# Cross-attention maxima pass from the keys' high parts, two heads on two halves of the array's rows

## The reference, cut to what matters

```python
q = (query @ w_q).reshape(B, Q, HEADS, HEAD_DIM).transpose(0, 2, 1, 3)
k = (key @ w_k).reshape(B, Kl, HEADS, HEAD_DIM).transpose(0, 2, 1, 3)
v = (value @ w_v).reshape(B, Kl, HEADS, HEAD_DIM).transpose(0, 2, 1, 3)
scores = jnp.einsum('bhqd,bhkd->bhqk', q, k) * scale
attn = jax.nn.softmax(scores, axis=-1)
out = jnp.einsum('bhqk,bhkd->bhqd', attn, v)
```

## Time and profile before

| what | value |
|---|---|
| three runs | 1546.65, 1551.68 and 1551.09 us, median 1551.09 |
| span of the profiled execution | 1543.7 us; its own time is not listed beside it, and the three runs are 3.0 to 8.0 us longer than this span |
| TensorE matmuls busy | 1382.7 us (90%) |
| VectorE busy | 1007.9 us (65%) |
| ScalarE busy | 886.8 us (57%) |
| GpSimd busy | 232.3 us (15%) |

### The profile page before, as it was taken

The page is one execution under the profiler, slowest core; times in us unless marked ns, Lnnn a source line. Parts: engine busy times, 40 slices in busy tenths (PEclk is TensorE's granted clock), DMA queues, the critical chain, the costliest instruction groups (busy, mean ns, idle before and its releaser), DMA issues. The chain is left out here.

```text
span 1543.7 us, 23087 instructions
## 1 busy us (share of the span) xinstructions
PE 1382.7 (90%) x8543; PEld 1040.3 (67%) x8543; DVE 1007.9 (65%) x1283; ACT 886.8 (57%) x1569; POOL 232.3 (15%) x214
## 2 busy tenths in 40 slices
PE   3999999999999998999999999999995999999653
PEld 3878786877777786877787777878783456355322
DVE  5657677685867676667767685767765656025376
ACT  3858576675758575757667585857661433023053
POOL 3202122120302111112112030211213000000000
PEclk9999999999999999999999999999996979569786
DMA  4000000000000013000000000000004151510000
GB/s 139 15 1 18 12 7 18 1 17 1 18 1 14 18 29 92 8 5 14 18 1 19 1 18 2 18 14 1 4 1 153 19 70 17 61 13 1 20 1 14
DMA packets 31717, 34.64 MB, mean 22 GB/s; under 512 B 2688, under 2 KB 28800, under 8 KB 31360
## 3 DMA queue, kind: packets, MB, share of 16 engines
q1 hardware_dynamic: 31616, 33.17, 9.5%
HBM read 25.82 MB, written 0.52 MB: 17 GB/s over the span
## 5 line engine op out<-in xcount | busy, mean ns | idle before, releaser
L459 DVE TENSOR_TENSOR prob_sum<-prob_sum,probs 128x1024 f32<-128x1024 f32 x224 | 264.5, 1222 | 164.6 <-ACT probs L382 163.9
L382 ACT ACTIVATE probs<-scores_a 128x1024 f32<-128x1024 f32 x128 | 131.2, 1025 | 209.1 <-PE scores_a L573 208.1
L311 POOL TENSOR_TENSOR k_split<-prob_sum,k_split 64x512 fp32r<-64x512 f32 x128 | 165.1, 1290 | 297.9 <-ACT prob_sum L358 297.9
L440 DVE TENSOR_REDUCE step_max<-scores_a 128x2 f32<-128x1024 f32 x128 | 156.9, 1226 | 35.4 <-PE scores_a L561 33.5
L440 DVE TENSOR_REDUCE step_max<-scores_b 128x2 f32<-128x1024 f32 x128 | 155.7, 1216 | 0.0
L572 PE MATMUL scores_a<-q_twice,k_split 128*128 128x256 f32 x512 | 139.2, 305 | 5.0 <-ACT q_low_max L373 4.9
L382 ACT ACTIVATE probs<-scores_b 128x1024 f32<-128x1024 f32 x128 | 131.3, 1026 | 0.0
L572 PE MATMUL scores_b<-q_twice,k_split 128*128 128x256 f32 x512 | 128.4, 283 | 0.0
L573 PE MATMUL scores_b<-q_low_max,k_ones 128*128 128x256 f32 x512 | 127.9, 282 | 0.0
L573 PE MATMUL scores_a<-q_low_max,k_ones 128*128 128x256 f32 x512 | 127.9, 283 | 0.0
L304 POOL TENSOR_TENSOR w_lo<-w_raw,w_hi 128x768 fp32r<-128x768 f32 x16 | 34.9, 2183 | 606.3 <-ACT w_hi L327 606.3
(11 more groups left out here) (210 smaller groups left out, 2784.1 us busy)
## 6 DMA issues: line engine op xcount, KB each, us to landing
ctx_rows<-in_ctx_dram SPq DMA_DIRECT2D x10, 512.0 KB, 3.7
grouped<-dots_sb SPq DMA_DIRECT2D x32, 136.0 KB
w_raw<-in_L_xattn_w_v_dram SPq DMA_DIRECT2D x14, 256.0 KB, 3.2
probs<-in_ctx_dram SPq DMA_DIRECT2D x6, 512.0 KB, 6.0
grouped<-dots_sb SPq DMA_DIRECT2D x32, 72.0 KB
w_raw<-in_L_xattn_w_q_dram SPq DMA_DIRECT2D x16, 128.0 KB, 2.4
w_raw<-in_L_xattn_w_k_dram SPq DMA_DIRECT2D x16, 128.0 KB, 2.4
wo_pair<-in_L_xattn_w_o_dram SPq DMA_DIRECT2D x16, 128.0 KB, 2.1
```

The costliest lines, as they stand in the source:

```text
L311: pool.tensor_tensor(k_split[0:DH, B, keys], k_staged_b[j % 2], k_split[DH:P, B, keys].bitcast(F32), ALU.subtract).then_inc(k_low[B], 1)
L382: act.activation(probs[:, j % 2, h, :], flat_scores[h], ACT.Exp, scale=SCALE).then_inc(exp_done, 1)
L440: dve.tensor_reduce(step_max[:, :, 1 - h, j - 1], scores[h][:, :, :], X, ALU.max).then_inc(max_done, 1)
L459: dve.tensor_tensor(prob_sum[:, h, :], prob_sum[:, h, :], probs[:, j % 2, h, :], ALU.add).then_inc(sum_done, 1)
```

## The change

The maxima pass multiplies only the high parts of queries and keys: head A on rows 0 to 63, head B on rows 64 to 127, where the high part of its keys lies. The matmuls are issued as A, B for the first half of the queries and A, B for the second. All waits stand ahead of the four matmuls: the pass waits for the high parts of the chunk (k_high) instead of the low ones, and for the reductions of both heads. The wait for the low parts moves to the first call of scores_by_keys for each head. Empty lines are left out of the diff.

```diff
             def scores_for_max(it, j):
                 keys = slice(j * CHUNK, (j + 1) * CHUNK)
+                pe.wait_ge(k_high, 2 * (STEPS * it + j) + 2)
                 for h in (A, B):
-                    pe.wait_ge(k_low[h], STEPS * it + j + 1)
                     if j > 0:
                         pe.wait_ge(max_done, 2 * (STEPS * it + j - 1) + h + 1)
                     else:
                         wait_past(pe, exp_done, 2 * STEPS * it)
-                    for qt in range(QT):
-                        last = mm(scores[h][:, qt, :], q_twice[:, h, qt * P:(qt + 1) * P], k_split[:, h, keys],
+                for qt in range(QT):
+                    for h in (A, B):
+                        rows = slice(h * DH, (h + 1) * DH)
+                        last = mm(scores[h][:, qt, :], q_twice[rows, h, qt * P:(qt + 1) * P], k_split[rows, h, keys],
                                   start=True, stop=True)
-                    last.then_inc(pre_made, 1)
+                        if qt == QT - 1:
+                            last.then_inc(pre_made, 1)
 
             def scores_by_keys(it, j, h):
 
                 if j > 0:
                     pe.wait_ge(exp_done, 2 * (STEPS * it + j - 1) + h + 1)
+                else:
+                    pe.wait_ge(k_low[h], STEPS * (it + 1))
                 for t in range(KT):
```

## The result

The changed kernel took **1574.17 us** in the median of 4 runs (1568.85 to 1575.44); the kernel before, on the same chip, 1548.87 (4 runs, 1526.43 to 1551.68). The ratio is 1.0203, with an interval of 1.0116 to 1.0290: slower, by some 25 us. The forecast was 1563, 12 us slower. The sign and the mechanism came out as forecast; the size was over twice the forecast one, and this part is about the other half. The ratios given in this document leave out the slower executions of each kernel, so they are not always the quotients of the medians beside them.

A forecast was written before the change was run, and what follows sets the result against it. TensorE sets most of the pace, in a loop with VectorE's reductions; 14 pairs at +0.85 us (11.9) and +0.1 in each of two first pairs give +12 on the 1551.1 median: 1563 us, range 1547 to 1575.

The forecast's parts named there:

- The bound, and the loop: Cross-attention pair: TensorE busy 32.70 of 34.00 us; scores banks refill only after their last reduction, which VectorE's next reduction needs.
- part 1: Scores for the maxima: A's and B's half-row matmuls run side by side, 0.47 us instead of 0.93.
- The rival without overlap: Scores for the maxima: A's and B's matmuls do not run at once; 1603 us, +52; chance 0.07.
- part 2: Array's division changes before and after each step's scores, 0.20 us each way; one call 0.87 us instead of 0.93.
- The rival in which row changes are free: Scores for the maxima: changing only rows costs nothing; 1543.7 us, faster; chance 0.12.
- the bound step of the walk: Where the reduction loop binds, one step takes 2.36 + 0.05 + 0.76 = 3.17 us, +0.06 in three steps.
- the walk: Step-by-step sum through one pair, between starts of A's reductions: last reductions +1.55 us, transpose of the maxima +0.85 us.
- steps 4 and 5: Fourth and fifth intervals between A's reductions in a pair: 3.69 us each, +0.34 and -0.06.
- part 4: Wait on k_low moves to the first scores_by_keys, k_high replaces it; neither binds, costed at nothing.
- the narrower value projection: Last pair of each batch: about the same loss as other pairs, counted in 14 x 0.85 = 11.9 us.
- a cheaper division: A division change costing less than 0.15 us, down to nothing: chance 0.30, 0.12 faster and 0.18 no difference.
- step 7: Last interval between A's reductions in a pair: the refill stands between them, 3.17 us instead of 2.27, +0.90.

The follow-up runs named there:

- run 5: The kernel before, with each reduction reading half of the scores (256 of 512 keys of each bank); 1520.85 us, one run.
- run 6: The changed kernel, with each reduction reading half of the scores; 1516.76 us, one run.
- run 7: The kernel before, full rows, with half a value projection between head A's and head B's scores from chunk 2 on; 1520.14 us, ratio 0.9857.
- run 9: The kernel of run 7 with both heads' scores on half rows, each head's two matmuls alone between value projections; 1600.37 us, one run.
- run 4: The changed kernel with one wait on the reductions (head B's, which includes A's) instead of two; 1578.49 us, ratio 1.0240.
- run 8: The changed kernel with the waits for the keys' low parts moved ahead of the transposes of the maxima; 1551.11 us, one run.
- run 1: The changed kernel with the last pair of each batch projecting its values at full width, 256 columns; 1556.65 us.
- run 3: The changed kernel, still on half rows, with the order and reduction waits of the kernel before; 1566.35 us, ratio 1.0128.
- run 2: The kernel before, on all 128 rows, with the change's order A, B, A, B and both heads' waits ahead; 1556.09 us, ratio 1.0054.

## Why the prediction was right or wrong

**The bound, and the loop: right.** The pair is set by the loop between the scores' banks and the reductions. Runs 5 and 6 take VectorE's part of the loop out, and the loss goes; run 7 hides the loop, and the pair gets 1.1 us shorter than before.

**The overlap (part 1): right.** The pairs start together, 402.07 and 402.08. The rival without overlap is out.

**The change of division (part 2): right, 0.20 forecast, 0.19 to 0.20 measured** in run 9, although it was read from changes of columns. In the changed kernel's rows the first reduction comes when forecast: the key projection's last matmul would have let the next start at 401.52 + 2 x 0.233 = 401.99, and 402.84 - 401.99 = 0.85 us, the forecast's own figure. The rival in which row changes are free is out with it. The Trainium skill (TensorEngine Tiling (Array Packing), Key Properties) says that a change of tiling mode drains the engine. The trace agrees in that each change costs 0.19 to 0.20 us, less than the forecast's estimate of 0.28 us for a full drain; that it is a drain, no run here shows. The Trainium skill (TensorEngine Tiling (Array Packing), Theoretical Speedup) gives up to twice for such a contraction; here two row pairs start 0.33 us apart where four full-row matmuls started 0.233 apart, and with both changes one call takes 0.85 instead of 0.93 us.

**The restart after a wait (the bound step of the walk): wrong in size.** The forecast took 0.05 + 0.76 = 0.81 us from the end of B's reduction to the next of A's. Measured: 0.15 + 0.74 = 0.89 (405.19, 405.34, 406.08). Its ground for part 2, that an empty array has nothing to drain, held: restarts with a change of division take as long as the late ones without (run 4). What failed is the 0.05, which was read at 403.52 in an ordinary pair of the kernel before, where the weight load carries the wait. The change puts more waits in front of the matmuls, and the one that ends last became an instruction of its own. The same trace had that price in its first pair, at 46.76. The four bound steps exceed the walk by 0.07 to 0.08 each, steps 4 and 5 by 0.04 and 0.02. Counted from 401.99, where the scores would have started without a change, the transpose comes after 28.01 us, where the forecast had 27.65: 0.36 more.

**The wait that moved (part 4): wrong.** "I cost it at nothing; the cover is the value projection." The cover held for the data, but not for the wait: 1.61 instead of 1.50 us from the transpose to the first scores by keys in every ordinary pair, 0.11 more, which run 8 finds between the release and the matmul. Both misses are one: the forecast priced waits by whether their data is there, and not by where they stand in TensorE's queue. An ordinary pair so loses 0.85 + 0.36 + 0.11 = 1.3 instead of 0.85. (The 0.85 hold the change in front of the first scores, 0.09 of which shows as 33.19 - 27.94 = 5.25 us from the first key projection to the first scores, where it was 5.16.)

**"With the narrower value projection the same walk gives about the same": wrong.** With wide projections and at a full clock these two pairs take 27.84 us from the scores to the transpose (run 1), as the others do; with the narrow ones it was 30.43. The forecast read a granted clock of 1.00 in the kernel before and took it as fixed, though the change thins TensorE's work. In the two last pairs it fell to the lower level, which cost 10.5 us in all. Seven kernels had half rows. Of these, the clock fell in both last pairs in the changed kernel and runs 3, 4 and 8, in one in run 9, and in none in run 1 (wider projections) and run 6 (short reductions, one wait left in such a pair). In the kernel before and in runs 2, 5 and 7, with full rows, it stayed. So it fell only where half rows and narrow projections came together, and not everywhere there; what decides is open, since in run 9 it fell without a wait just ahead and in run 6 it did not fall.

**The sum.** 15.3 in the 12 ordinary pairs, 10.5 for the clock and 2.0 for the rest of the two last pairs, 1.3 in the two first pairs, -0.6 at the start: 28.5 up to the end of the cross-attention, and +25 in the medians; the forecast's own terms gave 12. The range (1547 to 1575) held 1574.17 by a hair, and not by its reasons: it was widened by a cheaper division and by other small prices, while the clock was in none of its cases. Its 0.3% for what a measurement of this kernel tells was too small as well: the four runs of the kernel before lie between 1526.43 and 1551.68 us.

**After the transpose: nearly right.** Apart from the added wait, a pair's second stage takes as long as before (32.2 us in both kernels in about half of the pairs, up to 34 in the others), and the part behind the cross-attention too.

## What to carry to other kernels

Splitting the array pays only if what it takes off the engine is more than two changes of division per visit (0.4 us here), so few long visits should beat many short ones. When a resource is refilled and drained by two engines in turn, a wait that joins two staggered halves can cost most of the stagger (step 7 grew by 0.97 us, where the two reductions start 1.14 apart); a wait costs even when its data is long there, if it stands between a late release and what that releases; interleaving independent work between the halves, as in run 7, was worth more than halving the arithmetic. And where a change thins TensorE's work, its narrowest stage deserves a case of its own in the forecast, in which the granted clock falls.

## What the runs showed of the hardware that was not expected

- A change of the array's division cost 0.19 to 0.20 us between matmuls that follow one another without a wait (run 9), and nothing measurable at a restart after a wait (0.85 us from the release to the end of the second matmul, with it and without).
- One wait more in TensorE's queue, its condition long met, cost 0.09 to 0.11 us where it stood between a late release and the matmul that is released (0.15 instead of 0.05 at the restarts, 0.35 instead of 0.24 in front of the scores by keys). At the restarts 0.06 us of it are left at the end of the second matmul.
- Fewer rows and fewer columns per matmul brought the clock down to 1.2 GHz in a stretch in which the same instructions with twice the columns kept 2.4 GHz: 10.5 us lost by doing less.
- The part behind the cross-attention, untouched by all of these kernels, has a 40 us stretch that was seen at both levels of the clock. In the kernel before (its cross-attention ends at 1172.9):

```profile
1313.00:1353.00 40.00, 37.37 (x90) 16.20 (x90) 2.17 (x3) 3.55 (x8) 0.00 (x0) 0.55 0.58 61
```

and in version 7 (1156.3), at the same distance from that end:

```profile
1296.00:1336.00 40.00, 36.24 (x156) 20.98 (x155) 3.60 (x9) 4.32 (x10) 0.00 (x0) 0.96 0.58 62
```

90 matmuls in 40 us at 0.55, 156 at 0.96; the whole part takes 370.8 and 349.9 us. The changed kernel had 0.57 there, run 1 had 0.96. In run 3 the clock stayed at 1.00 there and fell to 0.59 between 1413 and 1453 us instead, and the part took 368.8 us. Of the 26 us between the medians of version 7 and the kernel before, only the 16.6 us of the cross-attention are shown to be its doing; what decides the level in that stretch was not tried.
